# Front of a two-layer fp32 kernel: low parts on one engine, a first chunk in two pieces, two load and split orders moved

## The chip, the cores and the metric

The kernel runs on one core of a Trainium2 chip. The time is device microseconds of one execution. The kernel is one hand-written program for five engines: PE (TensorE), DVE (VectorE), ACT (ScalarE), POOL (GpSimd) and SP (SyncE, which here only issues DMAs). Each engine runs its own list of instructions in order and waits on semaphores.

## What is computed

Four batches of 2048 tokens of 512 numbers, all fp32:

```
feats   = exp(x @ (ab * gs).T - 0.5 * |x|^2 * ab^2) * exp(ab) / sqrt(512)
weights = the same of input_weights (512 x 512)
x = layernorm(x + feats @ weights.T)
x = layernorm(x + sqrt((x @ cos(theta + theta_noise))^2 + (x @ sin(phi + phi_noise))^2))
```

## The kernel before

**Tiling.** The 8192 tokens are NB = 16 blocks of B = 512; every 512 x 512 matrix is C = 4 chunks of 128 partitions. Each product is kept near fp32 precision by three products of rounded parts: a matrix is split into a high part (`_hi`, a rounding to fp32r, by ACT as a copy) and a low part (`_lo`, the original less the high part, `lower` at L1288), and PE sums hi x hi, hi x lo and lo x hi.

**Stages.** The front (about the first 45 us) loads `gsT` and `wT` (in the tile `z`), and multiplies them chunk by chunk into four banks (L1026 to L1040): for chunk c four products of `gs_hi` with `zT_hi`, four of `gs_lo` with `zT_hi` (L1034), four of `gs_hi` with `zT_lo` (L1037). Ahead of them PE runs `WARM_UP = 9` small products on a tile of ones (L1024), each of two recorded pieces. `zT_hi` of chunk 0 is rounded by DVE (L1306), of the others by ACT (L623); `zT_lo` is made by POOL (L439), `gs_lo` by DVE (L1309). Then a sum of squares (L1049, L1050) and the projection of token block 0 (`xT_first`) follow, and block 0 and block 1 are done by `first_step` and `second_step`. In `first_step` PE projects the next block's four column groups, and group 2 waits for the first exponent of that block (L1114, `expo_made`), which DVE makes at L1293 from token norms: ACT sums squares (L593), DVE turns them, SP stores them to DRAM (L312) and fetches them back to all partitions (L316).

**Steady blocks.** From block 2 (`PLAIN`) the second layer uses seven quarter products `M1` to `M7` per pair of token tiles (`PAIRED_ORDER`, L254). `M7` waits for `half_sums_lo_made` (DVE, `split_half_sums`, L1645, a 128 x 1024 `lower`). `M6` is summed onto the bank of `M1`, so it waits for `first_copied` (ACT, `copy_first`, L854); ACT comes to that copy behind the four `features` of the step (L646, L647 each), and each feature pair waits for its exponent (DVE, `next_exponent`). `M3` waits for `W_copied` (ACT, `copy_W`, L864), behind two `sum_square` (L593) which read the tokens of a later block (`x_tok`). Block 2, called with `behind_plain=True`, has its own order on DVE and ACT.

**What sets the order.** The order in every engine's function is written by hand. SP's DMAs are issued in program order: in each step `x_tok` of block b + 2 (L380), then its columns `xT_raw` (L382), then two stores of the output. In the front SP issues four `gsT` chunks, four `xT_first` chunks, `xis`, four theta chunks (each behind its `gs_lo`), the tokens of block 1, then, behind the first `xT_hi`, the columns of block 1 and the tokens of block 0 and phi. POOL issues the accumulating loads of theta's and phi's noise (L444) and counts whole turns of the angles.

## Time and profile before

| | |
|---|---|
| time of 3 runs, median (lowest to highest) | 693.6 us (692.81 to 693.67) |
| the profiled execution | 692.88 us |
| its span, first to last instruction | 691.1 us |
| PE busy of the span | 681.6 us (99%) |
| DVE, ACT, POOL busy | 579.5, 482.8, 170.7 us |
| DMA | 90.23 MB, mean 131 GB/s |

Busy PE time is modelled (matmuls are pipelined), so 99% says only that PE nearly always had a product in hand. The chain of waits is the finer view: it lists how long each piece of PE's work took from the end of the piece before. A 512-column product takes 0.23 us in it, and a piece that takes longer has waited.

### The profile page before, as it was taken

To read this page: it belongs to the slowest core of one execution; us is meant where nothing else is said; L and a number is where in the kernel's file an instruction comes from. 1 tells how busy PE (TensorE), PEld (TensorE's weight loads), DVE (VectorE), ACT (ScalarE), POOL (GpSimd) and SP (SyncE) were. 2 spreads that over 40 slices of the span, in tenths; PEclk is the share of its full clock that TensorE was granted. 3 is DMA by queue.
4 is the path that set the end of the run, shared out by engine and by line. 5 is a ranking of instruction groups with operands and counts; after the bars stand their busy time and mean duration, and the time that the engine had idled before them with its cause. 6 is when DMAs were issued, how large, how long until landed. Compare 5 with 4: busy or idle time off the path is not lost.

```text
span 691.1 us, 10093 instructions
## 1 busy us (share of the span) xinstructions
PE 681.6 (99%) x3010; PEld 562.9 (81%) x3010; DVE 579.5 (84%) x903; ACT 482.8 (70%) x771; POOL 170.7 (25%) x240
## 2 busy tenths in 40 slices
PE   9999999999999999999999999999999999999995
PEld 8888888888888888888888888888888888888874
DVE  6788899888879798887969878797887979888877
ACT  6867998386585758668585776858667685866466
POOL 5772304103012040301304031130302104030205
PEclk9999999999999999999999999999999999999998
DMA  8862031471835538083653817456281654707142
GB/s 311 236 138 61 16 115 69 107 213 27 215 96 122 181 79 238 18 188 127 125 182 70 223 40 162 142 127 192 42 218 74 146 157 108 211 24 176 31 121 92
DMA packets 179302, 90.23 MB, mean 131 GB/s; under 512 B 121040, under 2 KB 149712, under 8 KB 179280
## 3 DMA queue, kind: packets, MB, share of 16 engines
q1 hardware_dynamic: 175328, 86.30, 46.4%
q0 software_dynamic: 1152, 2.10, 1.8%
q10 hardware_dynamic: 2800, 1.57, 0.8%
q8 instruction: 10, 0.16, 0.1%
q14 instruction: 12, 0.10, 0.0%
HBM read 58.46 MB, written 31.49 MB: 130 GB/s over the span
## 4 chain that ended last, share of the span: by engine, by line
PE 88%; DVE 5%; issue 4%; ACT 1%; DMA 1%; POOL 0%; SPq 0%; POOLq 0%; ACTq 0%; DVEq 0%
PE token_ps L1068 7%; PE token_ps L1070 7%; PE token_ps L1069 7%; PE token_ps L1181 6%; PE token_ps L1182 6%; PE token_ps L1183 6%; PE project_ps L1012 5%; PE project_ps L1014 4%; PE project_ps L1013 4%; PE project_ps L1181 4%; PE project_ps L1182 4%; PE project_ps L1183 4%; PE turn_ps L1012 4%; PE turn_ps L1014 4%; PE turn_ps L1013 4%
## 5 line engine op out<-in xcount | busy, mean ns | idle before, releaser
L505 POOL TENSOR_TENSOR plain_late<-z,plain_late 128x1024 f32<-128x1024 f32 x13 | 31.3, 2409 | 288.0 <-ACT plain_late L754 288.0
L1068 PE MATMUL token_ps<-W_hi,F_hi 128*128 128x512 f32 x240 | 93.4, 389 | 0.0
L1069 PE MATMUL token_ps<-W_lo,F_hi 128*128 128x512 f32 x240 | 93.4, 389 | 0.0
L1070 PE MATMUL token_ps<-W_hi,F_lo 128*128 128x512 f32 x240 | 93.4, 389 | 0.0
L760 ACT ACTIVATE o_tile<-plain_late,shift,rstd 128x512 f32<-128x512 f32 x56 | 42.8, 809 | 57.7 <-POOL shift L518 50.3
L1288 DVE TENSOR_TENSOR zT_lo<-plain_zT_lo,zT_hi 128x768 fp32r<-128x768 f32 (+1 forms) x54 | 58.9, 1090 | 6.6 <-ACT zT_hi L849 5.1
L646 ACT ACTIVATE F_hi<-plain_expo,ab 128x512 fp32r<-128x512 f32 x62 | 44.5, 718 | 24.1 <-DVE plain_expo L1293 24.0
L754 ACT ACTIVATE plain_late<-plain_late 128x1024 f32<-128x1024 f32 x28 | 29.6, 1057 | 42.2 <-POOL plain_late L501 39.3
L1012 PE MATMUL project_ps<-xT_hi,gs_hi 128*128 128x512 f32 x144 | 56.7, 394 | 0.0
L1014 PE MATMUL project_ps<-xT_hi,gs_lo 128*128 128x512 f32 x144 | 56.1, 390 | 0.0
L1013 PE MATMUL project_ps<-xT_lo,gs_hi 128*128 128x512 f32 x144 | 56.1, 389 | 0.0
L1288 DVE TENSOR_TENSOR xT_lo<-plain_xT_lo,xT_hi 128x1024 fp32r<-128x1024 f32 x28 | 49.4, 1802 | 6.4 <-ACT xT_hi L674 6.4
L1070 PEld LDWEIGHTS token_ps<-W_hi,F_lo 128*128 128x128 f32 x240 | 45.1, 188 | 9.4
L1068 PEld LDWEIGHTS token_ps<-W_hi,F_hi 128*128 128x128 f32 x240 | 45.1, 188 | 9.3
L1069 PEld LDWEIGHTS token_ps<-W_lo,F_hi 128*128 128x128 f32 x240 | 45.1, 188 | 9.3
L1288 DVE TENSOR_TENSOR F_lo<-plain_F_lo,F_hi 128x1024 fp32r<-128x1024 f32 (+1 forms) x38 | 42.2, 1139 | 3.5 <-ACT plain_F_lo L647 3.5
L1423 DVE TENSOR_TENSOR z<-token_ps,x_tok 128x512 f32<-128x512 f32 x60 | 40.9, 685 | 4.7 <-DVE stats L1394 1.4
L1012 PE MATMUL turn_ps<-xT_hi,gs_hi 128*128 128x512 f32 x112 | 44.0, 393 | 0.0
L647 ACT ACTIVATE plain_F_lo<-plain_expo,ab 128x512 f32<-128x512 f32 x62 | 44.0, 709 | 0.0
L1181 PE MATMUL token_ps<-T_hi,zT_hi 128*128 128x512 f32 x112 | 43.7, 390 | 0.1
L1014 PE MATMUL turn_ps<-xT_hi,gs_lo 128*128 128x512 f32 x112 | 43.6, 389 | 0.0
L1013 PE MATMUL turn_ps<-xT_lo,gs_hi 128*128 128x512 f32 x112 | 43.6, 389 | 0.0
(335 smaller groups left out, 1904.1 us busy)
## 6 DMA issues: line engine op xcount, KB each, us to landing
x_tok<-in_x SPq DMA_DIRECT2D x16, 1024.0 KB, 5.9
out_tokens<-o_tile SPq DMA_DIRECT2D x62, 256.0 KB, 3.2
plain_xT_lo<-in_xT SPq DMA_DIRECT2D x14, 1024.0 KB, 8.9
turned_pair<-plain_late SPq DMA_DIRECT2D x104, 128.0 KB, 2.8
plain_zT_lo<-turned_pair SPq DMA_DIRECT2D x27, 256.0 KB, 2.8
plain_zT_lo<-turned_pair SPq DMA_DIRECT2D x54, 128.0 KB, 2.9
norm_bc<-token_norms SPq DMA_DIRECT2D x15, 256.0 KB, 3.0
z<-in_wT ACTq DMA_DIRECT2D x4, 256.0 KB, 4.9
```

The lines of the kernel that those rows point to most:

```text
L646: nc.scalar.activation(F_hi[:, j, :], exponents, ACT.Exp, scale=ab[:, j:j + 1]).then_inc(exp_done, 1)
L647: nc.scalar.activation(F_raw[:, j, :], exponents, ACT.Exp, scale=ab[:, j:j + 1]).then_inc(exp_done, 1)
L1012: nc.tensor.matmul(o, gs_hi[:, c, cols], rhs_hi[:, c, :], start=(c == 0), stop=False)
L1013: nc.tensor.matmul(o, gs_hi[:, c, cols], rhs_lo[:, c, :], start=False, stop=False)
L1014: return nc.tensor.matmul(o, gs_lo[:, c, cols], rhs_hi[:, c, :], start=False, stop=(c == C - 1))
L1068: nc.tensor.matmul(o, F_hi[:, c, cols], W_hi[:, c, :], start=(c == 0), stop=False)
L1069: nc.tensor.matmul(o, F_hi[:, c, cols], W_lo[:, c, :], start=False, stop=False)
L1070: return nc.tensor.matmul(o, F_lo[:, c, cols], W_hi[:, c, :], start=False, stop=(c == C - 1))
L1181: nc.tensor.matmul(o, left[0][i], right[0][i], start=(i == 0 and not onto), stop=False, skip_group_check=onto)
L1182: nc.tensor.matmul(o, left[0][i], right[1][i], start=False, stop=False, skip_group_check=onto)
L1183: last = nc.tensor.matmul(o, left[1][i], right[0][i], start=False, stop=(i == H - 1), skip_group_check=onto)
L1288: return tt(dst, whole, hi.bitcast(F32), ALU.subtract)
```

## The change

- `WARM_UP` goes from 9 to 7.
- `gsT` chunk 0 is loaded in two DMAs (columns 0 to 127, then 128 to 511) and rounded by ACT in two instructions; PE's first product waits for the first piece alone.
- POOL's four `zT_lo` go to DVE, as `split_weights(c)`, the first ahead of `gs_lo` of chunk 0 and the others behind `gs_lo` of their chunk; PE takes `zT_lo` products ahead of `gs_lo` products.
- ACT's `AB` exponential goes from ahead of `split_hi(0, ...)` to its middle, behind two roundings of `xT_first`.
- PE's first projection waits for `xT_lo` chunk by chunk.
- In each step but the first, SP issues the columns `xT_raw` behind the two stores and behind the landing of `x_tok`.
- In block 2 DVE does `split_half_sums(b, 0)` ahead of `next_exponent(b, slot, 2)`.

```diff
-        WARM_UP = 9
+        WARM_UP = 7
...
+            sp.dma_start(gs_raw[:, 0, 0:P], by_chunk(gsT)[:, 0, 0:P]).then_inc(gs_first_loaded, 16)
             for c in range(C):
-                sp.dma_start(gs_raw[:, c, :], by_chunk(gsT)[:, c, :]).then_inc(gs_loaded[c], 16)
+                begin = P if c == 0 else 0
+                sp.dma_start(gs_raw[:, c, begin:], by_chunk(gsT)[:, c, begin:]).then_inc(gs_loaded[c], 16)
...
                 if ahead:
                     sp.wait_ge(y_made, C * (b + 1))
                     sp.dma_start(x_tok[:, slot], x_blocks[b + 2]).then_inc(x_loaded[slot], 16)
-                    sp.wait_ge(project_done, C * (b + 3))
-                    sp.dma_start(xT_raw[:, :, :], xT_blocks[b + 2]).then_inc(xT_loaded, 16)
+                    if first:
+                        sp.wait_ge(project_done, C * (b + 3))
+                        sp.dma_start(xT_raw[:, :, :], xT_blocks[b + 2]).then_inc(xT_loaded, 16)
                 if not first:
                     store_out(b - 1, 2)
                     store_out(b - 1, 3)
                 if ahead:
+                    if not first:
+                        sp.wait_ge(x_loaded[slot], 16 * (pair + 2))
+                        sp.wait_ge(project_done, C * (b + 3))
+                        sp.dma_start(xT_raw[:, :, :], xT_blocks[b + 2]).then_inc(xT_loaded, 16)
                     store_norms(b + 3, 1 - slot)
                     fetch_norms(b + 3, 1 - slot)
...
-            for c in range(C):
-                pool.wait_ge(wT_hi_made if c else wT_first_hi_made, max(c, 1))
-                pool.tensor_tensor(turned(zT_lo, c), z[:, c, :], turned(zT_hi, c).bitcast(F32), ALU.subtract).then_inc(wT_lo_made, 1)
...
                     if b == 0 and c == H:
+                        act.wait_ge(xis_loaded, 16)
+                        nc.scalar.activation(AB[:, :], ab[:, :], ACT.Exp).then_inc(AB_made, 1)
                         round_total(0, squares_summed, 3)
...
             for c in range(C):
+                if c == 0:
+                    act.wait_ge(gs_first_loaded, 16)
+                    nc.scalar.activation(gs_hi[:, 0, 0:P], gs_raw[:, 0, 0:P], ACT.Copy).then_inc(gs_first_hi_made, 1)
+                begin = P if c == 0 else 0
                 act.wait_ge(gs_loaded[c], 16)
-                nc.scalar.activation(gs_hi[:, c, :], gs_raw[:, c, :], ACT.Copy).then_inc(gs_hi_made, 1)
+                nc.scalar.activation(gs_hi[:, c, begin:], gs_raw[:, c, begin:], ACT.Copy).then_inc(gs_hi_made, 1)
...
-                pe.wait_ge(gs_hi_made, c + 1)
                 pe.wait_ge(wT_hi_made if c else wT_first_hi_made, max(c, 1))
                 for j in range(C):
+                    if c == 0 and j == 0:
+                        pe.wait_ge(gs_first_hi_made, 1)
+                    else:
+                        pe.wait_ge(gs_hi_made, c + 1)
                     nc.tensor.matmul(token_ps[j][:, :], gs_hi[:, c, cols[j]], turned(zT_hi, c), start=(c == 0), stop=False)
...
-            pe.wait_ge(xT_lo_made, C)
             first_project_ps = project_ps + turn_ps
-            project(0, first_project_ps[0])
+            for c in range(C):
+                pe.wait_ge(xT_lo_made, c + 1)
+                last = project_part(first_project_ps[0][:, :], c, 0, xT_hi, xT_lo)
+            last.then_inc(project_done, 1)
...
+            def split_weights(c):
+                dve.wait_ge(wT_hi_made if c else wT_first_hi_made, max(c, 1))
+                lower(turned(zT_lo, c), z[:, c, :], turned(zT_hi, c)).then_inc(wT_lo_made, 1)
+
+            split_weights(0)
             for c in range(C):
                 dve.wait_ge(gs_hi_made, c + 1)
+                if c == 0:
+                    dve.wait_ge(gs_first_hi_made, 1)
                 lower(gs_lo[:, c, :], gs_raw[:, c, :], gs_hi[:, c, :]).then_inc(gs_lo_made, 1)
+                if c:
+                    split_weights(c)
...
                 split_halves(b, 0)
+                if behind_plain:
+                    split_half_sums(b, 0)
                 next_exponent(b, slot, 2, wide_project_ps)
-                split_half_sums(b, 0)
+                if not behind_plain:
+                    split_half_sums(b, 0)
                 next_exponent(b, slot, 3, wide_project_ps)
```

The order of DVE's instructions in the front, before (`z` holds wT, `plain_T_hi` holds gsT):

```order
L1306 TENSOR_SCALAR zT_hi<-z 128x512
L1288 TENSOR_TENSOR gs_lo<-plain_T_hi,gs_hi 128x512 x4
L1313 TENSOR_TENSOR plain_expo<-plain_expo 128x512
L1315 TENSOR_TENSOR plain_late<-plain_late 128x512
L1317 TENSOR_TENSOR plain_expo<-plain_expo,plain_late 128x512
```

And of the changed kernel:

```order
L1319 TENSOR_SCALAR zT_hi<-z 128x512
L1301 TENSOR_TENSOR zT_lo<-z,zT_hi 128x512
L1301 TENSOR_TENSOR gs_lo<-plain_T_hi,gs_hi 128x512 x2
L1301 TENSOR_TENSOR zT_lo<-z,zT_hi 128x512
L1301 TENSOR_TENSOR gs_lo<-plain_T_hi,gs_hi 128x512
L1301 TENSOR_TENSOR zT_lo<-z,zT_hi 128x512
L1301 TENSOR_TENSOR gs_lo<-plain_T_hi,gs_hi 128x512
L1301 TENSOR_TENSOR zT_lo<-z,zT_hi 128x512
L1337 TENSOR_TENSOR plain_expo<-plain_expo 128x512
```

Four `zT_lo` are new on DVE, three of them between the `gs_lo`.

DVE in block 2, before, from the second exponent of the step on (`plain_expo` is the exponent, the 768-wide `zT_lo` is `split_halves`, the 1024-wide one `split_half_sums`):

```order
L1293 SCALAR_TENSOR_TENSOR plain_expo<-norm_bc,neg_half_ab,project_ps 128x512
L1288 TENSOR_TENSOR zT_lo<-plain_zT_lo,zT_hi 128x768
L1293 SCALAR_TENSOR_TENSOR plain_expo<-norm_bc,neg_half_ab,turn_ps 128x512
L1288 TENSOR_TENSOR zT_lo<-plain_zT_lo,zT_hi 128x1024
L1293 SCALAR_TENSOR_TENSOR plain_expo<-norm_bc,neg_half_ab,turn_ps 128x512
```

And of the changed kernel:

```order
L1306 SCALAR_TENSOR_TENSOR plain_expo<-norm_bc,neg_half_ab,project_ps 128x512
L1301 TENSOR_TENSOR zT_lo<-plain_zT_lo,zT_hi 128x768
L1301 TENSOR_TENSOR zT_lo<-plain_zT_lo,zT_hi 128x1024
L1306 SCALAR_TENSOR_TENSOR plain_expo<-norm_bc,neg_half_ab,turn_ps 128x512 x2
```

The 1024-wide split now stands ahead of both last exponents of the step.

## Rows read from the trace of the kernel before

**Rows 1.** The page: busy time, share of the span and instructions of each engine.

```profile
PE 681.6 (99%) x3010; PEld 562.9 (81%) x3010; DVE 579.5 (84%) x903; ACT 482.8 (70%) x771; POOL 170.7 (25%) x240
```

**Rows 2.** Chain of waits, first 8 us: start us, us, what.

```profile
1.05 4.21 PE turn_ps L1024 x18
...
5.26 1.61 PE token_ps L1031 x4
6.87 0.91 PE token_ps L1034 x4
```

**Rows 3.** Timeline, 3.9 to 6.9 us: start us, us, engine, line, operation, tiles, idle before.

```profile
2.70 1.28 ACT L620 ACT_TABLE_LOAD   x1 [2.70 <-issue]
...
4.04 0.43 DVE L1306 TENSOR_SCALAR zT_hi<-z 128x512 fp32r<-128x512 f32 x1 [2.77 <-DMA z<-in_wT]
```

**Rows 4.** Timeline of DVE and ACT in the front, 6 to 17 us.

```profile
8.39 0.69 DVE L1288 TENSOR_TENSOR gs_lo<-plain_T_hi,gs_hi 128x512 fp32r<-128x512 f32 x1 [1.42 <-ACT gs_hi L620]
...
10.72 1.78 DVE L1313 TENSOR_TENSOR plain_expo<-plain_expo 128x512 f32<-128x512 f32 x1
...
12.28 0.21 ACT L626 ACTIVATE AB<-ab 128x4 f32<-128x4 f32 x1 [1.31 <-DMA ab<-in_xis]
...
13.93 0.63 ACT L605 ACTIVATE expo<-plain_expo 128x512 fp32r<-128x512 f32 x1 [0.40 <-DVE plain_expo L1317]
```

**Rows 5.** Timeline, 34 to 46 us: phi's noise, the norms, the exponent.

```profile
34.76 3.55 POOL L444 DMA_DIRECT2D plain_late<-in_phi_noise  x4
...
35.86 1.29 SPq L312 DMA_DIRECT2D token_norms<-norm_row  x4
41.18 0.35 SPq L316 DMA_DIRECT2D norm_bc<-token_norms  x1
...
45.45 0.75 DVE L1293 SCALAR_TENSOR_TENSOR plain_expo<-norm_bc,neg_half_ab,project_ps 128x512 f32<-128x512 f32 x1 [0.45 <-DMA norm_bc<-token_norms]
```

**Rows 6.** Chain of waits, 46 to 47 us: PE's third projection of `first_step`.

```profile
46.37 0.39 PE project_ps L1012
```

**Rows 7.** Timeline, 13.2 to 13.5 us: theta's noise between two loads of SP.

```profile
13.03 0.38 SPq L357 DMA_DIRECT2D plain_T_hi<-in_xT  x1
...
13.28 1.07 POOL L444 DMA_DIRECT2D plain_T_hi<-in_theta_noise  x1 [1.32 <-DMA plain_T_hi<-in_theta]
```

**Rows 8.** Chain of waits, 143 to 146 us: PE from M1 to M7 in block 2.

```profile
144.61 0.10 issue
144.70 0.47 PE token_ps L1181
```

**Rows 9.** Timeline of DVE and ACT in block 2, 141 to 148 us.

```profile
142.68 0.74 DVE L1293 SCALAR_TENSOR_TENSOR plain_expo<-norm_bc,neg_half_ab,turn_ps 128x512 f32<-128x512 f32 x1
143.34 1.22 DVE L1288 TENSOR_TENSOR zT_lo<-plain_zT_lo,zT_hi 128x1024 fp32r<-128x1024 f32 x1
144.47 0.75 DVE L1293 SCALAR_TENSOR_TENSOR plain_expo<-norm_bc,neg_half_ab,turn_ps 128x512 f32<-128x512 f32 x1
...
143.67 0.71 ACT L646 ACTIVATE F_hi<-plain_expo,ab 128x512 fp32r<-128x512 f32 x1
...
145.25 0.72 ACT L646 ACTIVATE F_hi<-plain_expo,ab 128x512 fp32r<-128x512 f32 x1 [0.26 <-DVE plain_expo L1293]
...
146.49 0.57 ACT L854 ACTIVATE plain_late<-token_ps 128x512 f32<-128x512 f32 x1
```

**Rows 10.** Timeline of PE's weight loads in block 2: M1's last, M7's and M6's first.

```profile
144.00 0.19 PEld L1183 LDWEIGHTS token_ps<-cos_hi,zT_lo 128*128 128x128 f32 x1
144.67 0.19 PEld L1181 LDWEIGHTS token_ps<-T_hi,zT_hi 128*128 128x128 f32 x1 [0.49 <-issue]
...
147.28 0.19 PEld L1181 LDWEIGHTS token_ps<-T_hi,zT_hi 128*128 128x128 f32 x1
```

**Rows 11.** Timeline of ACT, 231 to 235 us: block 4.

```profile
232.57 0.63 ACT L593 ACTIVATE unused<-x_tok 128x512 f32<-128x512 f32 x1 [0.36 <-DMA x_tok<-in_x]
```

**Rows 12.** Chain of waits, 234 to 236 us: M3 of block 4 begins.

```profile
234.71 0.38 PE token_ps L1181
```

More of the change, by code:

```diff
@@ L362, in _, with step @@
             fetch_norms(2, 0)
-            def step(b, slot, ahead, first=False, moved=False, behind_plain=False):
+            def step(b, pair, slot, ahead, first=False, moved=False, behind_plain=False):
                 if moved:
@@ L400, in _ @@
             for slot in range(2):
-                step(PLAIN + slot, slot, True, moved=True, behind_plain=(slot == 0))
+                step(PLAIN + slot, 1, slot, True, moved=True, behind_plain=(slot == 0))
             with sp.Fori(2, NB // 2 - 1) as pair:
                 for slot in range(2):
-                    step(pair * 2 + slot, slot, True, moved=True)
-            step(NB - 2, 0, False, moved=True)
+                    step(pair * 2 + slot, pair, slot, True, moved=True)
+            step(NB - 2, NB // 2 - 1, 0, False, moved=True)
             last = NB - 1
@@ L624, in _ @@
                 square_columns(0, c, z)
-            act.wait_ge(xis_loaded, 16)
-            nc.scalar.activation(AB[:, :], ab[:, :], ACT.Exp).then_inc(AB_made, 1)
             split_hi(0, xT_first)
```

13 lines of the change are left out of this document (7 added, 6 removed).

## The prediction

> **What bounds the kernel now.** First the page: PE is busy for 681.6 of the span of 691.1 us, no other engine is over 84% [rows 1]. So time is won only where PE waits or runs slowly, and lost only where PE is made to wait. The next view is the chain of waits, in short windows: the reader is to look for pieces of PE that take more than the usual 0.23 us. The change touches four such places, and the first three quarters of the trace show hardly any other. At the front four products take 1.61 us, 0.40 each, and the next four 0.91, 0.227 each [rows 2]: 512 columns in 0.227 us fits the upper level of the clock, 2.4 GHz, and 0.40 is the lower one, 1.2 GHz (0.427), with the rise to the upper inside the last product. The other places are 46.4 us (0.39 instead of 0.23, so 0.16 lost) [rows 6], block 2's M7 (0.10 + 0.47, so 0.34 lost) [rows 8], and block 4's M3 (0.38, so 0.15 lost) [rows 12]. All that the change can win is thus about one microsecond.
>
> The sum is made against the profiled execution, 692.88 us. The median of the runs shown is 693.6, 0.7 higher; the same difference is applied to it.
>
> **The start.** The warm-up takes 4.21 us for 18 pieces, 0.234 each, and ends at 5.26 [rows 2]; four pieces fewer end at about 4.3. What PE then needs: ACT's table load ends at 2.70 + 1.28 = 3.98 [rows 3], and the first piece of `gs_hi` follows. A rounding of 512 columns takes 0.63 and an activation of 4 columns 0.21 [rows 4]; a quarter of the way gives 0.31, so it is ready near 4.29, if its load has landed. `zT_hi` is ready at 4.04 + 0.43 = 4.47 [rows 3], and comes last. Before, the first product ended at 5.26 + 0.427 = 5.69. A product that PE had waited for, M7's first, ended at 144.70 + 0.47 = 145.17, 0.61 behind its release by DVE at 143.34 + 1.22 = 144.56 [rows 8, 9]; at the lower level a product is 0.2 longer, so the first one now ends near 4.47 + 0.82 = 5.29. PE is 0.4 ahead, but in a stretch at half pace: 0.4 / 0.427 is 0.94 of a product, worth 0.227 each once the clock has risen. I take -0.21. The bounds are 0 (the second piece of chunk 0 lands too late; its issue comes 0.4 us later, as issues of SP last 0.38 [rows 7], and PE needs it for its second product) and -0.4 (the rise of the clock comes sooner by as much).
>
> **Low parts on DVE.** DVE gets four more instructions of 0.69 [rows 4]. Three of them lie in the time in which it waited for ACT (1.42 idle at 8.39 alone [rows 4]). The fourth stands ahead of the sums of squares, +0.6; but the first of these sums took 1.78 beside POOL's last `zT_lo`, and would take 0.69 [rows 4], -1.1. So the sums end some 0.5 sooner, and ACT, which stood idle 0.40 for them [rows 4], follows. `AB` stays hidden: ACT sat idle 1.31 for `xis` ahead of it [rows 4], and now uses that time for two roundings. PE is not reached by any of this: without POOL, `gs_lo` and `zT_lo` are there before their products. If this cover failed, each late low part would cost up to 0.7. The wait for `xT_lo` by chunks stands at a place without a long piece: nothing. So 0, with -0.1 and +0.7 as bounds.
>
> **At 46 us.** PE lost 0.16 to an exponent, and the exponent sat 0.45 behind the landing of the norms [rows 5, 6]. Four small stores issued from 35.86 on were answered only at 41.18, beside phi's noise, issued at 34.76 [rows 5]. If the norms don't come sooner, all that was won ahead of this place is given back here. Two things push them: ACT and DVE are about 0.5 ahead; and SP issues the columns of block 1 and the tokens of block 0 over a microsecond sooner (they wait for the first `xT_hi`, now no longer behind `xis`), ahead of theta's noise, where they stood around it [rows 7]. If what is issued first is served first, theta's noise, POOL's turns and then phi's noise come later, and the norms' stores run free. I take -0.16 and keep the start's gain; the other end, +0.21, gives the start back.
>
> By the Trainium skill, DMA: Bandwidth & Descriptors, section "Queues, rings and completion order", each DMA engine goes round-robin between the queues that have work, so POOL's noise would not be pushed back by what SP issued earlier. By that rule the norms keep their place beside phi's noise, and the sum would be that of the second rival.
>
> **Block 2.** `split_half_sums` now begins where the exponent did, 142.68, and 1.13 later the next can begin (143.34 to 144.47) [rows 9]. It ends at 143.90, before M7 asks at 144.00 + 0.23 [rows 10]: the 0.34 goes. But the third exponent moves from 142.68 to 143.81 and ends at 144.55. ACT, which began the third features at 143.67, now begins at 144.58. The fourth exponent is ready at 145.2 as before; a features pair takes 1.24 (145.25 to the copy at 146.49), so the fourth begin at 145.82 and the copy of M1, `copy_first`, at 147.06 instead of 146.49 [rows 9]. It ends at 147.63. M6 waits for that copy. Its first weight load stood at 147.28 with the copy done at 147.06 [rows 9, 10], 0.22 of margin; with M7's wait gone PE asks at 146.94, and is held 0.7. M7's weight load was 0.44 late for 0.34 of loss [rows 8, 10], so 0.1 of a delay is absorbed, and about 0.63 is lost. Block 2 in all: -0.34 + 0.63 = **+0.29**. DVE and ACT follow PE into this block, so an earlier front doesn't change the spacing. Bounds: -0.34 (the copy is in time) and +0.4 (nothing absorbed).
>
> **Columns behind the tokens.** In block 4 ACT sat 0.36 for `x_tok` [rows 11], its later copy came late, and M3 lost 0.15 [rows 12]. With 1 MB of columns held back the tokens land sooner: -0.15, or 0 if they are late all the same. The columns land later; ACT rounds them at the end of the step, behind all its squares, which hides some microseconds; if that cover failed, the next projection would wait for the rest. SP's two stores come sooner, and the norms behind the columns are made only at the step's end. In the other steady blocks no long piece stands at M3: 0.
>
> **Sum:** -0.21 - 0.16 + 0.29 - 0.15 = -0.23: 692.65 for the profiled execution, **693.3** for the median (693.6 - 0.23, rounded down).
>
> **Rivals.** (1) *The move in block 2 works as it reads.* M6's copy is in time, because something in ACT's row is shorter than I laid out. Then -0.21 - 0.16 - 0.34 - 0.15 = -0.86: 692.7. For it: the margin missed is 0.7 us on a chain of two engines. Against: both work in order, with measured lengths. (2) *The norms hold the front.* The wait at 46 us grows by what was won: +0.29 - 0.15 = +0.14: 693.7. For it: the 0.45 of idle time ended by a landing. (3) *Slower: the clock.* PE worked without a break from 1.05 until the rise. Now PE idles for some 0.2 to 0.5 us between 4.3 and its first product, still at the lower level. If that puts the rise off, each microsecond of delay costs 1 - 0.227 / 0.427 = 0.47. The sum is then -0.23 + 0.47 for each: slower than before from 0.5 us of delay on, and +1.4, 695.0, at 3.5. I price it at that. For it: nothing in this trace shows a gap ahead of the rise; against: the gap is short beside the unbroken work around it.
>
> On that the Trainium skill, TensorE: Matmul & The Clock Gate, section "What's actually happening", says that the slow state is the default and that activity releases it; no row here shows how a short gap counts, so by the page alone the later rise and the forecast both stay open.
>
> **How the numbers follow.** Forecast 0.50, rival 1 0.17, rival 2 0.16, rival 3 0.10, something in the steady blocks that I don't see 0.07. The runs of before spread over 0.86 us, so each case is about 0.4 wide to either side. The range 692.4 to 694.3 holds all but rival 3 and the tails, and the bound of +0.7 for a late low part. Less than 0.2%, 1.4 us, can't be told from no change. Faster than that needs rival 1 and a bound or two (0.07), slower needs rival 3 or an unseen wait (0.09), the same 0.84.
>
> **What would show it.** Right: the first 512-column product ends near 5.3, the rise still comes near 6.7 (rival 3: microseconds later), L1012's successor near 46 us takes 0.23 (rival 2: over 0.39); in block 2 M7 begins without a wait and M6's first product takes about 0.85, behind ACT's `copy_first` (rival 1: 0.23); ACT no longer sits for `x_tok`. Wrong: M6 without a wait, or a long piece of PE where before there was none.

## The result, and the profile after

The changed kernel takes 695.87 us in the median of 12 runs (694.1 to 698.31); the kernel before takes 693.14 in the 12 runs beside it (692.1 to 694.55). The ratio is 1.0039, with a 95% interval of 1.0025 to 1.0053: 2.7 us slower. Forecast were 693.3 us with a range of 692.4 to 694.3, and a chance of 0.09 for slower by over 0.2%. So the prediction was wrong, in size and in sign. Four lone slow runs (860 to 3959 us, three of the kernel before and one of a kernel below) stand in none of the ratios and ranges.

The profiled execution took 695.64 us, with a span of 693.8, 2.7 more than before. Busy times, as in [rows 1]:

```profile
PE 682.8 (98%) x3006; PEld 562.6 (81%) x3006; DVE 581.3 (84%) x907; ACT 482.5 (70%) x772; POOL 165.6 (24%) x236
```

The four products fewer are the shorter warm-up, and the low parts went from POOL to DVE. Where the time went is seen in the chain of waits of the start, beside [rows 2] (start us, us, what):

```profile
1.31 3.90 DMA plain_T_hi<-in_gsT
...
5.23 0.53 ACT gs_hi L630
...
5.81 1.65 PE token_ps L1042 x3
7.46 1.71 PE token_ps L1045 x4
9.16 1.08 PE token_ps L1048 x4
```

And in the timeline of the same stretch (start us, us, engine, line, operation, tiles, idle before), beside [rows 3]:

```profile
3.99 0.31 ACT L627 ACTIVATE gs_hi<-plain_T_hi 128x128 fp32r<-128x128 f32 x1
...
4.45 0.77 PE L1042 MATMUL token_ps<-zT_hi,gs_hi 128*128 128x512 f32 x1
5.23 0.52 ACT L630 ACTIVATE gs_hi<-plain_T_hi 128x384 fp32r<-128x384 f32 x1 [0.93 <-DMA plain_T_hi<-in_gsT]
```

The first product ends at 5.22. Then PE stands still: the second piece of chunk 0, issued at 1.31, lands after 3.90 us, and its rounding ends at 5.75. From there each product takes 0.43 (1.71 for the four of L1045), the lower level of the clock, 1.2 GHz. Only inside the first product of L1048, the ninth of all, which takes 0.38, does the clock rise, near 9.5. In [rows 2] it rose inside the fourth, near 6.8. The ninth product ended at 8.0 before and ends at 9.54 now. These 1.5 us are over half of what this execution loses (2.7).

The rest, read from PE's pieces that take more than 0.23 us:

| place | before | after |
|---|---|---|
| up to the ninth product | | +1.54 |
| 46 us, third projection | 0.16 lost | none |
| block 2, M1 | none | 0.62 lost |
| block 2, M7 | 0.34 lost | none |
| block 2, M6 | none | 0.72 lost |
| block 4, M3 | 0.15 lost | none |
| block 5, M3 | none | 0.45 lost |

The sum is +2.7, that of the two profiled executions. The table is of one execution each; some of these waits come and go between executions, as the experiments show. M6's wait is the chain that the prediction laid out (in the order of time, block 2):

```profile
144.74 1.22 DVE zT_lo L1301
145.95 0.67 DVE plain_expo L1306
...
146.65 0.72 ACT F_hi L654
147.37 0.61 ACT plain_F_lo L655
147.98 0.61 ACT F_hi L654
148.60 0.61 ACT plain_F_lo L655
149.21 0.49 ACT plain_late L862
...
149.74 0.50 PE token_ps L1194
```

The 1024-wide split is at 144.74, the exponent behind it, two features pairs behind that, then `copy_first` (L862), and M6's first product behind the copy. M3's wait of block 5 has tokens at its root, as block 4's had in [rows 11], but longer (timeline of ACT, and the chain behind it):

```profile
276.06 0.63 ACT L597 ACTIVATE unused<-x_tok 128x512 f32<-128x512 f32 x1 [0.66 <-DMA x_tok<-in_x]
```

```profile
277.54 0.49 ACT plain_late L872
...
278.07 0.50 PE token_ps L1194
```

### The profile page after: what moved, and what is told of

Read it like the earlier page. It is cut to its first block, busy times and chain, and to the rows that moved or that the text cites. A ratio compares the mean times of both kernels' runs of the same rounds, so it can differ in the third digit from the quotient of the medians.

```text
span 693.8 us, 10095 instructions
## 1 busy us (share of the span) xinstructions
PE 682.8 (98%) x3006; PEld 562.6 (81%) x3006; DVE 581.3 (84%) x907; ACT 482.5 (70%) x772; POOL 165.6 (24%) x236
## 4 chain that ended last, share of the span: by engine, by line
PE 79%; DVE 7%; issue 4%; DMA 4%; ACT 2%; SPq 2%; POOL 1%; POOLq 0%; ACTq 0%; DVEq 0%
PE token_ps L1083 7%; PE token_ps L1082 7%; PE token_ps L1081 7%; PE token_ps L1194 5%; PE token_ps L1196 5%; PE token_ps L1195 5%; PE project_ps L1020 4%; PE project_ps L1022 4%; PE project_ps L1021 4%; PE project_ps L1196 4%; PE project_ps L1195 4%; PE project_ps L1194 4%; PE turn_ps L1022 3%; PE turn_ps L1021 3%; PE turn_ps L1020 3%
## 5 line engine op out<-in xcount | busy, mean ns | idle before, releaser
L1196 PE MATMUL token_ps<-T_hi,zT_lo 128*128 128x512 f32 x112 | 43.6, 389 | 0.0
```

What stands on the lines that cost most here:

```text
L1196: last = nc.tensor.matmul(o, left[1][i], right[0][i], start=False, stop=(i == H - 1), skip_group_check=onto)
```

## The experiments

Each kernel was timed beside the kernel before, whose medians there were 693.2 to 693.6 us; ratios are to it, with 95% intervals.

**Undoing parts of the change.** Each of these is the changed kernel with one edit.

```diff
-        WARM_UP = 7
+        WARM_UP = 9
```

> The changed kernel with WARM_UP = 9 again, all else of the change in place. Theory 1 (the idle PE delays the clock's rise): in the changed kernel PE idled between the warm-up's end at 4.4 us and the second product of chunk 0, which began only near 6.2. Now the warm-up fills this up to 5.3, the second product waits only until some 5.8, the rise comes near 6.7 again instead of 9.4, and the time falls by (9.4 - 6.7) x 0.47 = 1.3 us, to about 694.6. Theory 2 (the rise falls where it will in each execution, and the 2.7 us come from waits in blocks 2 and 5): no change beyond 0.2 us against 695.9.

Measured: 696.0 us in the median (693.13 to 696.88), ratio 1.0036 [1.0025, 1.0047]. Its profiled execution (694.26) shows the rise near 6.4, as the first theory has it, and PE only 0.2 us behind the kernel before at 93 us instead of 1.4. But the median didn't fall, and the profiled execution is the second fastest of the twelve, so it doesn't stand for the median. The clock is then not the only cost: with PE at full pace, it next waits for chunk 1 (0.39 us here, 1.07 in another kernel below), and in block 11 M3 waits 1.0 us. Whether the clock rose late in the slower executions of this kernel isn't known.

```diff
-            sp.dma_start(gs_raw[:, 0, 0:P], by_chunk(gsT)[:, 0, 0:P]).then_inc(gs_first_loaded, 16)
             for c in range(C):
-                begin = P if c == 0 else 0
-                sp.dma_start(gs_raw[:, c, begin:], by_chunk(gsT)[:, c, begin:]).then_inc(gs_loaded[c], 16)
+                sp.dma_start(gs_raw[:, c, :], by_chunk(gsT)[:, c, :]).then_inc(gs_loaded[c], 16)
```

> The changed kernel with chunk 0 of gsT loaded and rounded in one piece, WARM_UP still 7. PE idles in one stretch, from 4.4 to the rounding's end near 4.9, about 0.5 us, instead of the 0.1 and 1.0 us of the changed kernel. Theory 1: if the idle time's length matters the rise comes between 6.7 and 9.4, the time 694.5 to 695.9; if any idle time does, 695.9. Theory 2: 695.9 less the 0.2 us of a second product that no longer waits. A third reading (the second piece is landed late, and this alone costs the time, without the clock) gives about 695.0.

Measured: 696.75 (694.97 to 699.41), 1.0049 [1.0032, 1.0067]. PE idles once, from 4.40 to 5.48, and the rise comes at 10.3. The rise is thus late without the piecewise load too; what the two kernels share is over 1 us of idle time ahead of it.

```diff
                 split_halves(b, 0)
-                if behind_plain:
-                    split_half_sums(b, 0)
                 next_exponent(b, slot, 2, wide_project_ps)
-                if not behind_plain:
-                    split_half_sums(b, 0)
+                split_half_sums(b, 0)
```

> The changed kernel with split_half_sums of block 2 behind the third exponent again, as before. In the changed kernel's trace M6 waited 0.72 us there and M7 not at all (0.34 before). By these two the time falls by 0.72 - 0.34 = 0.38 us, to about 695.5, with M7's first product at about 0.57 and M6's at 0.23. If the wait of M1 in the same block (0.62 us in the changed kernel, 0 before) hangs on the move too, it goes as well and the time is about 694.9. A theory under which block 2 costs nothing in the end gives 695.9.

Measured: 697.48 (694.25 to 700.56), 1.0051 [1.0031, 1.0071], which is no gain. M6's wait is gone and M7's is back at 0.43 us, as written. But M1 of block 2 waits 1.09, and in two steady blocks M3 waits 1.69 and 0.85 us, both behind late tokens. The wide spread of the kernels that hold the columns back was the sign to look there.

**Doing one part alone.** Each of these is the kernel before with one edit.

```diff
-        WARM_UP = 9
+        WARM_UP = 7
```

> The kernel before with WARM_UP = 7 alone. PE idles from 4.4 to about 4.9 us before its first product, nothing else is moved. Theory 1: the rise comes later than 6.6 us and all up to it runs at 0.427 us a product; for a rise near 9.4 the kernel is 1.3 us less the 0.2 won at the start slower than before, about 694.2; Theory 2: within 0.2 us of the kernel before, 693.1.

Measured: 695.12 (693.98 to 696.38), 1.0026 [1.0017, 1.0036]. Ten products run at the lower level, the rise comes near 9.8 (chain of waits):

```profile
0.87 3.39 DMA plain_T_hi<-in_gsT
...
4.29 0.64 ACT gs_hi L620
...
4.97 2.07 PE token_ps L1031 x4
7.04 1.71 PE token_ps L1034 x4
8.75 1.40 PE token_ps L1037 x4
```

The warm-up ends at 4.40, `gs_hi` is there at 4.93. This one number, changed alone, costs 1.8 us.

```diff
-                    sp.wait_ge(project_done, C * (b + 3))
-                    sp.dma_start(xT_raw[:, :, :], xT_blocks[b + 2]).then_inc(xT_loaded, 16)
+                    if first:
+                        sp.wait_ge(project_done, C * (b + 3))
+                        sp.dma_start(xT_raw[:, :, :], xT_blocks[b + 2]).then_inc(xT_loaded, 16)
                 if not first:
                     store_out(b - 1, 2)
                     store_out(b - 1, 3)
                 if ahead:
+                    if not first:
+                        sp.wait_ge(x_loaded[slot], 16 * (pair + 2))
+                        sp.wait_ge(project_done, C * (b + 3))
+                        sp.dma_start(xT_raw[:, :, :], xT_blocks[b + 2]).then_inc(xT_loaded, 16)
```

> The kernel before with one edit: from the second step on, SP issues the columns behind the two stores and behind the landing of the tokens. In four profiles with this order ACT stood idle for x_tok 0.65 to 1.86 us in one or two steady blocks each, and M3 behind it lost 0.45 to 1.69 us; in two profiles without it only once 0.36 us. Theory A (the order itself makes the tokens land late in some blocks): about 1 us slower than the kernel before in the median, 694.3, with a wider spread, and the profile shows a long M3. Theory B (late tokens come by chance, whatever the order): equal to the kernel before within 0.2 us, 693.3. By the prediction's term: 0.15 us faster.

Measured: 694.88 (692.74 to 697.75), 1.0021 [1.0009, 1.0034]. Theory A holds. The profile has three late landings (ACT idle 1.64, 0.65 and 0.35 us), and M3 loses 1.43, 0.45 and 0.16 behind them. The first, timeline of SP and ACT:

```profile
184.23 0.47 SPq L380 DMA_DIRECT2D x_tok<-in_x  x1
184.74 0.98 SPq L327 DMA_DIRECT2D out_tokens<-o_tile  x2
192.88 0.39 SPq L391 DMA_DIRECT2D plain_xT_lo<-in_xT  x1
```

```profile
192.89 0.63 ACT L598 ACTIVATE unused<-x_tok 128x512 f32<-128x512 f32 x1 [1.64 <-DMA x_tok<-in_x]
```

The same block of the kernel before, with the tokens issued at nearly the same time:

```profile
184.38 0.47 SPq L380 DMA_DIRECT2D x_tok<-in_x  x1
184.90 0.51 SPq L382 DMA_DIRECT2D plain_xT_lo<-in_xT  x1
185.44 1.20 SPq L327 DMA_DIRECT2D out_tokens<-o_tile  x2
```

```profile
191.31 0.62 ACT L593 ACTIVATE unused<-x_tok 128x512 f32<-128x512 f32 x1
```

There ACT begins at 191.31 without a wait. From the start of the issue to the landing the tokens take 5.9 us there, and 8.6 with the columns held (DMA views). The DMA view of the kernel with the edit, 184 to 194 us in 40 slices of 0.25 us (each digit the busy share of the 16 engines in tenths):

```profile
DMA  7999969518944988998898999999321211211211
```

From 191.25 on the digits are 3, 2 and 1, and mostly three data packets are under way at a time, where there were 15 to 17 at once before: three of the 16 engines are still at work with tokens and stores, while the others are done. ACT waits for those three until 192.87. By the Trainium skill, DMA: Bandwidth & Descriptors, section "Queues, rings and completion order", one copy is split over up to 16 engines' rings; the digits agree, and ACT waits for the last of them.

```diff
                 if behind_plain:
+                    split_half_sums(b, 0)
                 next_exponent(b, slot, 2, wide_project_ps)
-                split_half_sums(b, 0)
+                if not behind_plain:
+                    split_half_sums(b, 0)
```

> The kernel before with one edit: in block 2 the half sums ahead of the third exponent. The prediction's term: M7's wait of 0.34 us goes, M6 waits 0.63 behind ACT's copy, +0.29 us: 693.6. In the changed kernel M6 waited 0.72, with WARM_UP = 9 0.46: +0.1 to +0.4. A rival: the exponents made later also delay the squares and the DMAs of the next block and cost more than M6 shows, over 694.

Measured: 693.69 (692.67 to 694.09), 1.0004 [0.9995, 1.0013]. M7 doesn't wait, M6 loses 0.52 us behind the copy. That is +0.2 in block 2. The interval can't tell it from nothing, but it excludes a gain of over 0.4 us and a loss of over 0.9. (The trace as a whole is 0.9 us longer than that of the kernel before; 0.7 of it stands at 18 us, ahead of the edit's place, where PE's first projection waits for `xT_lo`.)

**Leaving out all but one part.** The changed kernel with WARM_UP 9 and the columns as before:

```diff
-        WARM_UP = 7
+        WARM_UP = 9
...
-                    if first:
-                        sp.wait_ge(project_done, C * (b + 3))
-                        sp.dma_start(xT_raw[:, :, :], xT_blocks[b + 2]).then_inc(xT_loaded, 16)
+                    sp.wait_ge(project_done, C * (b + 3))
+                    sp.dma_start(xT_raw[:, :, :], xT_blocks[b + 2]).then_inc(xT_loaded, 16)
...
-                    if not first:
-                        sp.wait_ge(x_loaded[slot], 16 * (pair + 2))
-                        sp.wait_ge(project_done, C * (b + 3))
-                        sp.dma_start(xT_raw[:, :, :], xT_blocks[b + 2]).then_inc(xT_loaded, 16)
```

> The changed kernel with WARM_UP = 9 and with the columns again right behind the tokens; left of the change are the two-piece chunk 0, the low parts on DVE, the projection by chunks and the half sums of block 2. Theory A: the spread of 693.1 to 696.9 that the changed kernel with WARM_UP = 9 had shrinks, and the time falls by about 1 us from its 696.0, to 694.9 or less. Theory B: no change, 696.0, and the loss sits in what is left. What the profiles show of what is left: the wait for chunk 1 at 9 us, 0.39 us, and M6's 0.46 against M7's 0.34, less the 0.16 at 46 us: +0.35 on 693.3, so 693.7 if nothing else is there.

Measured: 694.01 (693.03 to 695.28), 1.0012 [1.0003, 1.0021], 2 us less than with the columns held, and no late tokens in its trace. What remains is the front, where the two-piece chunk 0 has a cost of its own. Chain of waits at chunk 1:

```profile
1.78 6.27 DMA plain_T_hi<-in_gsT
...
8.07 0.63 ACT gs_hi L625
8.71 0.53 ACT zT_hi L628
...
9.28 1.21 PE token_ps L1037 x4
```

PE lost 1.07 us before these products. Chunk 1, now the third load of SP, was issued at 1.78 and landed at 8.05. ACT began its rounding at 8.07; in the trace of the kernel before it did at 5.55, in the changed kernel at 6.51, and in the changed kernel with WARM_UP 9 at 7.62. In all thirteen profiles with chunk 0 in one piece ACT began it between 5.41 and 5.75; in the four with two pieces at 6.51, 7.56, 7.62 and 8.07. So the third load of `gsT` in place of a second makes this landing late by 0.8 to 2.7 us, and only a PE at full pace has to wait for it.

Low parts on DVE, `AB` in the middle, projection by chunks, and nothing else; against the kernel before:

```diff
-            for c in range(C):
-                pool.wait_ge(wT_hi_made if c else wT_first_hi_made, max(c, 1))
-                pool.tensor_tensor(turned(zT_lo, c), z[:, c, :], turned(zT_hi, c).bitcast(F32), ALU.subtract).then_inc(wT_lo_made, 1)
...
+            split_weights(0)
             for c in range(C):
                 dve.wait_ge(gs_hi_made, c + 1)
                 lower(gs_lo[:, c, :], gs_raw[:, c, :], gs_hi[:, c, :]).then_inc(gs_lo_made, 1)
+                if c:
+                    split_weights(c)
```

> Of the change only this is left: the low parts of the weights on DVE instead of POOL (and PE's products in that order), AB in the middle of the split, the first projection by chunks. WARM_UP is 9, chunk 0 is one piece, columns and half sums stand as before. If the long pieces of the changed kernel come from its other parts, PE's front is as before up to 45 us and the wait of 0.16 at 46 us is gone: 0.16 us faster than the kernel before, 693.1. If the low parts come late behind each other on DVE, PE waits up to 0.7 us for one of them: 693.9. If the wait at 46 us was not ended by this but by the late clock of the changed kernel, it stays: 693.3.

Measured: 693.05 (692.27 to 693.75), 0.9997 [0.9989, 1.0006]: no difference to be told. PE never waits for a low part of the weights. The wait at 46 us is gone, but one of 0.26 us has appeared at 40 (chain of waits):

```profile
40.18 0.49 PE project_ps L1009
```

The same 0.26 at 40 us, and none at 46, is in the trace of the kernel above that only holds the columns, whose front is that of the kernel before. So this wait moves and vanishes between executions, and one profile without it shows no gain.

**Why the tokens come late.** In `step`, the stores ahead of the columns, without a wait for the landing (the edit is shown against the kernel that holds the columns):

```diff
                 if ahead:
                     if not first:
-                        sp.wait_ge(x_loaded[slot], 16 * (pair + 2))
                         sp.wait_ge(project_done, C * (b + 3))
```

> The kernel before, in each step but the first with the columns issued behind the two stores, but without a wait for the tokens' landing: tokens, two stores, columns. In the profile of the kernel with the whole edit the tokens of one block were issued at 184.23 us, as in the kernel before (184.38), and landed at 192.9 instead of before 191.3; 3 of the 16 DMA engines worked 1.7 us longer than the others. Theory C (the stores next behind the tokens make them late): as with the whole edit, 694.9 in the median, and a long M3 in one or two blocks. Theory D (holding the columns until the landing makes them late): as the kernel before, 693.3.

Measured: 693.89 (692.42 to 697.39), 1.0015 [1.0000, 1.0030]. ACT was idle for tokens in three blocks (0.46, 0.95 and 1.36 us), and M3 lost 0.26, 0.74 and 1.16. So the hold on the landing isn't needed for late tokens. The median lies between the two theories, but the three highest runs (695.83 to 697.39, the profiled one is the lowest of the three) are as slow as with the whole edit.

The other order, tokens alone, then columns, then stores (against the same kernel; the two stores that stood ahead of these lines are gone from there):

```diff
                     if not first:
                         sp.wait_ge(x_loaded[slot], 16 * (pair + 2))
                         sp.wait_ge(project_done, C * (b + 3))
                         sp.dma_start(xT_raw[:, :, :], xT_blocks[b + 2]).then_inc(xT_loaded, 16)
+                        store_out(b - 1, 2)
+                        store_out(b - 1, 3)
```

> The kernel before, in each step but the first with this order: tokens, wait for their landing, columns, two stores. Nothing is in flight behind the tokens. Theory C (the stores next behind the tokens make them late): the tokens land soonest of all, no M3 waits, the time is that of the kernel before, 693.3, or up to 0.15 us less. Theory D (holding the columns until the landing makes them late): as with the whole edit, 694.9, with late tokens.

Measured: 693.32 (692.38 to 695.45), 1.0006 [0.9997, 1.0015], and no idle time of ACT for tokens in any block. The block that was late above:

```profile
184.08 0.47 SPq L380 DMA_DIRECT2D x_tok<-in_x  x1
189.89 0.37 SPq L391 DMA_DIRECT2D plain_xT_lo<-in_xT  x1
```

SP, waiting for the landing, goes on at 189.89, 5.3 us behind the end of the issue. This profile is of the fastest of the eleven runs (692.38), and the intervals of the three orders overlap, so these two experiments alone would not decide. All profiles together do: in the six kernels with the two stores right behind the tokens (1 MB to read with 512 KB to write beside it) ACT waited for tokens in one to three steady blocks, and the latest landing came 7.4 to 8.2 us behind the end of its issue; in the eleven others it came at 6.0 to 7.0, and ACT waited once, 0.36 us in the kernel before. So it goes with the stores' place and not with the columns' delay. Why the columns in that place do less harm than the stores isn't shown; no view tells what one engine's lag comes from.

**What puts the clock's rise off.** Warm-up of 7, begun later, so that PE has no long idle stretch:

```diff
-        WARM_UP = 9
+        WARM_UP = 7
             pe.wait_ge(ones_made, 1)
+            pe.wait_ge(ident_made, 2)
```

> The kernel before with WARM_UP = 7 and the warm-up held until POOL has made its identity tile (near 1.8 us instead of 1.05): 14 pieces of 0.234 then end near 5.1, and PE stands idle only for 0.2 us before its first product, instead of 0.93 us as with WARM_UP = 7 alone, which ran all products up to 9.8 at the lower clock. If it is the idle stretch that puts the rise off: the rise comes about 0.8 us later than in the kernel before, near 7.4, and the time is 0.8 x 0.47 = 0.4 us above 693.3, so 693.7. If the amount of warm-up work decides (14 pieces are too few, 18 enough): the rise comes near 9.8 again, and the time is that of WARM_UP = 7 alone, 695.1.

Measured: 694.21 (693.26 to 695.09), 1.0014 [1.0005, 1.0023]. Four products at the lower level, rise by 7.2, with 14 pieces and 0.25 us of idle time behind them: so it isn't the number of pieces. The time is 0.5 above the first theory's; the trace has two waits that it left out, 0.52 at 47.5 us and 0.53 at M1 of block 2. The full warm-up, with an idle stretch added:

```diff
-                pe.wait_ge(gs_hi_made, c + 1)
+                pe.wait_ge(gs_hi_made, c + 1 if c else 2)
```

> The kernel before, warm-up untouched (18 pieces, 1.05 to 5.26 us), but the first product waits until ACT has rounded two chunks of gsT instead of one (6.18 us in its trace). PE thus stands idle for 0.93 us, as long as with WARM_UP = 7 alone, and everything else starts 0.93 us late. If the idle stretch puts the rise off: the rise comes near 10.5, and the time is 0.93 + 1.6 = 2.5 us above 693.2 less what chunk 1 no longer waits for: 695 to 695.7. If the amount of work ahead decides: the rise comes by 7 us and the time is at most 0.9 us above, 694.1.

Measured: 695.34 (693.97 to 698.56), 1.0029 [1.0018, 1.0041]. Timeline of PE:

```profile
4.20 1.06 PE L1024 MATMUL turn_ps<-plain_ones 128*128 128x128 f32 x4
6.40 2.07 PE L1031 MATMUL token_ps<-zT_hi,gs_hi 128*128 128x512 f32 x4 [1.14 <-ACT gs_hi L620]
```

PE's last warm-up piece ended at 5.26 and the first product, 0.43 long, at 7.19: 1.5 us idle, more than was planned. The rise comes near 10.6, though all 18 pieces were run. (The profiled execution is the slowest of the eight; it also has a wait of 1.8 us at 44.6, for `xT_lo` of DVE.) The middle size:

```diff
-        WARM_UP = 9
+        WARM_UP = 8
```

> The kernel before with WARM_UP = 8: PE stands idle for about 0.45 us between 4.85 and 5.3. In the runs so far 0.1 to 0.3 us of idle time left the rise at 6.0 to 7.2, and 0.9 us put it to 9.4 or later. If any idle time of some tenths of a microsecond puts the rise off: near 10, and 694.5 to 695. If this short one doesn't: rise by 7.2, time within 0.2 us of 693.2.

Measured: 694.54 (693.3 to 696.0), 1.0017 [1.0008, 1.0026]. PE was idle for 0.49 us, from 4.83 on, and the rise was not put off:

```profile
4.96 1.48 PE L1031 MATMUL token_ps<-zT_hi,gs_hi 128*128 128x512 f32 x4
```

The four take 1.48 (with the gap: 2.07), the last three 0.23 each, so the rise came by 5.75. What this kernel loses is elsewhere: 0.69 at 18 us, 0.48 at M1 of block 2, to which the next experiment belongs, and 1.2 near 635 us. At 18 us (timeline of PE) the first projection waits for all four `xT_lo`:

```profile
17.64 0.50 PE L1012 MATMUL project_ps<-xT_hi,gs_hi 128*128 128x512 f32 x1 [0.42 <-DVE xT_lo L1288]
```

Three of the ten profiles with this wait for all four lose 0.45 to 0.69 here (one more 0.1), none of the seven that project by chunks.

Each kernel has one profile, so none of them alone excludes a chance rise of the clock. All 17 together (both kernels and the 15 experiments) are plain: PE idle up to 0.57 us in twelve, 0.9 or more in five, and no exception in the rise.

**M1's wait in block 2.** M1 needs halves of the turned squares, which SP stores and fetches back. SP's four stores (timeline of SP), kernel before, WARM_UP 7 alone, changed kernel:

```profile
128.95 2.24 SPq L333 DMA_DIRECT2D turned_pair<-plain_late  x4
```

```profile
130.23 3.13 SPq L333 DMA_DIRECT2D turned_pair<-plain_late  x4
```

```profile
130.30 3.21 SPq L334 DMA_DIRECT2D turned_pair<-plain_late  x4
```

One of the issues takes a microsecond longer. The second store, kernel before and changed kernel:

```profile
129.32 0.56 SPq L333 DMA_DIRECT2D turned_pair<-plain_late  x1
```

```profile
130.67 1.57 SPq L334 DMA_DIRECT2D turned_pair<-plain_late  x1
```

The DMA view of the changed kernel, 129.5 to 132.5 us in 40 slices, has a lone packet there, of the queue of instructions:

```profile
DMA  0000000000000090000000489999999521000000
...
q8 instruction: 1, 0.02, 2.5%
```

It is a fetch of 16 KB. Outside the loop of steady blocks its queue's fetches lie 216 to 310 of PE's instructions apart, so I take it for PE's own; no view names the engine.

```diff
-        WARM_UP = 9
+        WARM_UP = 7
-            pe.wait_ge(ones_made, 1)
+            for _ in range(8):
+                pe.wait_ge(ones_made, 1)
```

> The kernel before with WARM_UP = 7 and eight waits for the tile of ones where there was one, so that PE's program keeps about the length that it had with WARM_UP = 9. In all five profiles with WARM_UP = 7 a fetch of 16 KB of instructions began at 129.9 to 131.3 us, right at the four stores of block 2's first squares (one issue of SP then lasted 1.1 to 1.6 us), and M1 of block 2 waited 0.3 to 1.1 us; in the nine with WARM_UP = 9 it began 0.4 to 0.8 us ahead of the first store, and M1 never waited. If the length of PE's program sets where the fetch falls: here it falls ahead of the stores again, M1 doesn't wait, and the time is 0.6 us below that of WARM_UP = 7 alone, 694.5. If the late start of the front sets it: M1 waits again and the time is 695.1. The rise comes late in both cases (PE stands idle for about 0.5 to 0.9 us).

Measured: 694.04 (693.33 to 694.58), 1.0008 [0.9999, 1.0017], 1.1 less than WARM_UP 7 alone. M1 doesn't wait, and the stores take 2.43:

```profile
129.19 2.43 SPq L333 DMA_DIRECT2D turned_pair<-plain_late  x4
```

Not all of it is M1's doing: the waits held the warm-up back, so PE idled 0.57 us instead of 0.93, and the rise came at 7.5, not late as was expected of both theories. The kernels with another warm-up or start, side by side (times in us; PE's lag is against the kernel before, read at 92.9 us there; a piece is two instructions, a weight load and a matmul; the eight waits became four instructions more, and the wait for the identity tile is one more):

| kernel | PE's instructions fewer | PE's lag | fetch begins | first store | the four stores | M1 loses |
|---|---|---|---|---|---|---|
| before | 0 | 0 | 128.2 | 128.95 | 2.24 | 0 |
| 9, with the gap | 0 | 4.2 | 132.4 | 133.16 | 2.25 | 0 |
| 7, eight waits | 4 | 0.3 | 128.9 | 129.19 | 2.43 | 0 |
| 8 | 4 | 0.5 | 129.2 | 129.36 | 2.95 | 0.48 |
| 7, begun later | 7 | 0.7 | 129.9 | 129.68 | 3.15 | 0.53 |
| 7 alone | 8 | 1.3 | 130.4 | 130.23 | 3.13 | 0.61 |
| changed kernel | 8 | 1.4 | 130.6 | 130.30 | 3.21 | 0.62 |

Fetch less lag is 128.2 without fewer instructions, 128.6 to 128.7 with 4 fewer, 129.1 to 129.2 with 7 or 8 fewer. Eight instructions are four products of 0.227 us: a fetch that hangs on a place in PE's program comes 0.9 us later when they are gone. The latest start of all, the kernel with the gap, has no stall and no wait, so it isn't the late front. That the fetch causes the longer issue is inferred, but in all 17 profiles the two go together: in the six where the fetch begins 0.2 us or less ahead of the first store, or behind it, one issue takes 1.1 to 1.6 us, in the eleven where it begins 0.3 us or more ahead, at most 0.75. Near 620 us a fetch begins among the four stores of a later block in every profile, and one issue takes 1.3 to 2.0, in the kernel before too (fetch at 620.28, timeline of SP):

```profile
620.29 1.55 SPq L333 DMA_DIRECT2D turned_pair<-plain_late  x1
```

There M1 doesn't wait in the kernel before, so a longer issue need not cost time.

**A version that beats both.** The low parts on DVE with their companions and block 2's half sums early, all else as before, and ACT's copy of M1 moved ahead of the last features pair:

```diff
                 features(C * (b + 2) + 2, 2, 0)
+                if behind_plain:
+                    copy_first(b, 0, 0, parts[:, 0], **how)
                 features(C * (b + 2) + 3, 3, 1)
-                copy_first(b, 0, 0, parts[:, 0], **how)
+                if not behind_plain:
+                    copy_first(b, 0, 0, parts[:, 0], **how)
```

> The version that the results point to: the low parts on DVE, WARM_UP 9, chunk 0 in one piece, columns right behind the tokens, block 2's half sums ahead of the third exponent, and new in it, ACT's copy of M1 in block 2 ahead of the fourth features pair instead of behind it, so that M6 needn't wait for it. M7's wait of 0.34 goes, the copy ends near 146.4 instead of 147.6 and M6 has its operands when PE comes at 146.9. With the 0.2 of the low parts: 693.3 - 0.2 - 0.34 = 692.8. If the features pair, now 0.57 later, is waited for by DVE and then PE, or M6 waits for something else, it comes out at 693.1 to 693.7.

Measured: 692.39 (691.5 to 693.03), 0.9986 [0.9977, 0.9995], so 0.3 to 1.6 us faster than the kernel before (0.8 by the medians). Timeline of ACT, and two pieces of the chain of waits, M7's first product and M6's:

```profile
145.18 0.57 ACT L851 ACTIVATE plain_late<-token_ps 128x512 f32<-128x512 f32 x1
145.66 0.71 ACT L643 ACTIVATE F_hi<-plain_expo,ab 128x512 fp32r<-128x512 f32 x1
```

```profile
144.04 0.23 PE token_ps L1183
...
146.76 0.23 PE token_ps L1183
```

The copy ends at 145.75, a microsecond ahead of M6, and neither product waits. How the gain is shared between this and the low parts isn't shown.

## Why the prediction was wrong, step by step

**The start** is the step that failed most in the traces. Its first half was right: the first product was put at 5.29 and ended at 5.22. The step then took the idle time as half-paced time won and set the rise where it had been ("a stretch at half pace: 0.4 / 0.427 ... I take -0.21"). Two things were wrong in it. The second piece's landing was a bound only (0), while it was the case: it landed 3.90 us behind its issue, and PE idled 0.4 us ahead of the first product and 1.0 ahead of the second (each product taken as 0.43 long). And the rise was moved by at most as much as PE was sooner, while it came 2.7 us later. In the sum stands -0.21; the ninth product shows +1.54.

**Rival 3, the clock**, was the mechanism, with its price of 0.47 for each microsecond of delay: (9.5 - 6.8) x 0.47 is 1.3, and the trace gives 1.5. The rest is the idle time ahead of the second product, 1.0 us at half pace, worth 0.5, less 0.25 for the first product's earlier start. The chance of 0.10 rested on "the gap is short beside the unbroken work around it". That was an opinion, no row. The runs order it: PE idle for 0 to 0.57 us ahead of the rise left it at 7.5 or before (twelve kernels), 0.9 us and more in sum put it to 9.5 to 10.6 (five kernels). Two of these five, 7 alone and 9 with the gap, have no other part of the change, so none of those is needed for a late rise. The gap that the rival priced, 0.2 to 0.5 us ahead of the first product, would by these runs have left the rise in time; with the late second piece PE idled for 1.4 us in sum. By the Trainium skill, TensorE: Matmul & The Clock Gate, section "Part 1: The HAM clock gate (the "warmup" mystery)", activity sets the clock and not the count of products; the rise by 7.2 with 14 pieces and 0.25 us of gap, and that near 10.6 with 18 and 1.5 us, agree.

**Low parts on DVE**: right. With its companions alone it is 0.9997 [0.9989, 1.0006]. In that kernel the first sum of the weights' squares took 0.68 instead of 1.78 [rows 4], and DVE was done with the sums at 13.0 instead of 13.8, 0.8 us sooner against 0.5 forecast; in the changed kernel, with its late chunks, at 13.9. The step called the place of the projection by chunks one without a long piece; in the trace before it was, but three other profiles lose 0.45 to 0.69 there, so this part may be worth more than nothing.

**At 46 us** the wait went, as forecast (-0.16). The reason given was not the one: in the changed kernel the norms were stored at 37.25 and fetched at 42.95, 1.4 and 1.8 us later than in [rows 5], and the exponent simply was DVE's next work:

```profile
46.30 0.73 DVE L1306 SCALAR_TENSOR_TENSOR plain_expo<-norm_bc,neg_half_ab,project_ps 128x512 f32<-128x512 f32 x1
```

It waits for nothing, as PE and DVE were late themselves. So the term came true by luck: the ten profiles with the low parts as before lose nothing to 0.5 us between 40 and 48 us, and 1.8 in one; the seven with them on DVE 0 in five, 0.17 and 0.26 in two. One reading of 0.16 was a draw from these. Rival 2 (the norms hold the front) is neither shown nor excluded.

**Block 2**: the mechanism was right, with M7 at no wait and M6 behind `copy_first`. The sum was +0.29; measured are -0.34 + 0.72 = +0.38 in the changed kernel and -0.34 + 0.52 = +0.18 with this part alone. What the step left out is that another part of the change, four pieces of warm-up fewer, moves the fetches of instructions, and with them M1: +0.62. The rows read had no price for it. The trace before does show the fetch 0.8 us ahead of these stores, and near 620 us one that falls on such stores and has an issue 1 us longer beside it.

**Columns behind the tokens** failed in sign: -0.15 forecast, +1.5 us measured alone (1.0021 [1.0009, 1.0034]). The step asked what the columns do to the tokens, and took no account of what takes their place right behind them, though it had the sentence for it: "SP's two stores come sooner". It should have been costed as a move of the stores too. In the medians this part alone misses by about as much as the start does, and taken out of the changed kernel with WARM_UP 9 it gives back 2.0 us (696.0 to 694.0). It also read one wait of 0.15 in one execution as a fixed cost; of the eleven profiles without the stores behind the tokens it is the only one in which ACT waits for them.

The parts don't add up in the medians: -0.2 (low parts), +0.3 (block 2), +1.8 (warm-up) and +1.5 (columns) make 3.4 before the two-piece chunk, and 2.7 were measured. The front may account for it in part: PE either waits for chunk 1 at full pace or is too slow to wait for it, and the changed kernel with WARM_UP 9 was no faster in the median. The changed kernel with nothing but the columns put back, which would divide the loss between the start and the columns, was not run.

Left open: M1 and M7 of a late block, near 635 us, lose 0.5 to 1.2 us in four profiles (`WARM_UP` 7, 8, 7 with eight waits, 9 with the gap), 0.1 to 0.3 in three others and at most 0.06 in the rest, the kernel before and the changed kernel among them, though in all of them a fetch falls on the stores ahead. And why single DMA engines lag.

## What to carry to other kernels

A warm-up should reach to the first real product: here an end half a microsecond early did the clock no harm, one a microsecond early kept it low for three more, and an operand in pieces opens such a gap again unless the second piece is there in time. When a DMA is moved back to free another one, cost what moves up into its place just as well, and look at many landings of the one that is freed, not at one. A profile of an edit that seems to cost only at its own place should be compared at the far end too: fewer instructions on an engine shift its fetches of instructions, and these can meet an issue on which everything waits.

## What the runs showed of the hardware that was not expected

A gap of 0.9 us and more in PE's work, ahead of the clock's rise, moved the rise from 6.8 us to between 9.5 and 10.6, while 0.5 to 0.6 us left it at 7.5 or before. A load of 384 columns by 128 partitions (192 KB) took 3.90 us to land beside the others of the front, and chunk 1, issued 0.47 us later, up to 6.27. An issue of SP took 1.1 to 2.0 us instead of 0.56 where a fetch of 16 KB of instructions began beside it. And one landing of tokens was held up by three of the 16 DMA engines, which worked 1.6 us longer than the others.
